# Audio tower on one core: the layers' attention in a new order, and the first stage's maxima subtracted by four wide products

## The reference

```
h = silu(xm @ W_h + b_h) @ W_o + b_o + xm @ W_r + b_r     # xm: 16 samples and 16 ones per token

def _L0_attn_ref(x):                                      # on layernorm(h), 16 heads of 16
    x_centered = xh - jnp.mean(xh, axis=1, keepdims=True)
    corr = jnp.einsum('bthd,bThd->bhtT', x_centered, x_centered)
    corr = jax.nn.softmax(corr, axis=-1)
    out = jnp.einsum('bhtT,bThd->bthd', corr, xh)
h = h + that

def _layer(x, ...):                                       # twice, on layernorm(h); 8 heads of 64
    h = shift_token(x)                                    # columns 128.. come from the token before
    q, k, v = jnp.split(h @ wqkv, 3, axis=-1)
    q = l2norm(q) * qs
    k = l2norm(k) * ksc
    q, k = rotary_xpos(q, k)
    o = local_attention(q, k, v)                          # causal, in a window; softmax(8 q k)
    x = x + o @ wo
    h = layernorm(shift_token(x)) * lg + lb
    a, g = jnp.split(h @ w1 + b1, 2, axis=-1)
    x = x + (a * gelu(g)) @ w2 + b2
h = h + that
```

## Time and profile before

| what | us |
|---|---|
| median of 3 runs (2812.47 to 2817.98) | 2816.48 |
| the profiled execution | 2815.47 |
| its span | 2813.7 |
| TensorE busy | 2682.4 (95%) |
| VectorE busy | 2019.9 (72%) |
| ScalarE busy | 1713.8 (61%) |
| GpSimd busy | 1414.7 (50%) |

### The profile page before, as it was taken

How to read it: one execution, slowest core, us unless ns; L and a number is a source line. 1 busy time by engine, 2 the same in 40 slices (tenths; PEclk the granted TensorE clock), 3 DMA queues, 4 the chain that set the end, 5 groups by cost and what they waited for, 6 DMA issues and landing times.

```text
span 2813.7 us, 68420 instructions
## 1 busy us (share of the span) xinstructions
PE 2682.4 (95%) x23682; PEld 2303.7 (82%) x23808; DVE 2019.9 (72%) x3899; ACT 1713.8 (61%) x4309; POOL 1414.7 (50%) x1337
## 2 busy tenths in 40 slices
PE   6999999968999999997999998999999999899998
PEld 5888888856888888886888886888888888788887
DVE  5666666638888888886755555888888888566664
ACT  3566666536777777775444443777777777444442
POOL 7777777659666666664100004866666666000000
PEclk9999999989999999999999999999999999999999
DMA  1011111021111111111211111111111111222221
GB/s 30 29 34 34 33 33 33 32 80 48 38 36 39 39 39 34 39 39 59 69 56 55 55 57 39 46 39 34 39 39 39 35 38 42 72 78 78 71 78 45
DMA packets 149226, 130.42 MB, mean 46 GB/s; under 512 B 23110, under 2 KB 147304, under 8 KB 149077
## 3 DMA queue, kind: packets, MB, share of 16 engines
q1 hardware_dynamic: 146773, 119.87, 14.1%
q0 software_dynamic: 2304, 8.47, 1.0%
HBM read 77.54 MB, written 50.33 MB: 45 GB/s over the span
## 4 chain that ended last, share of the span: by engine, by line
PE 70%; SPq 2%; DVE 2%; issue 2%; ACT 1%; DMA 0%; POOL 0%; DVEq 0%; ACTq 0%; POOLq 0%
PE const_banks L1292 6%; PE const_banks L1281 6%; PE const_banks L1283 6%; PE const_banks L1294 6%; PE const_banks L1282 6%; PE const_banks L1293 6%; PE const_banks L1375 5%; PE const_banks L1360 4%; PE const_banks L1385 4%; PE const_banks L1348 4%; PE const_banks L1404 3%; PE const_banks L1405 3%; PE const_banks L1406 3%; PE const_banks L1337 2%; PE const_banks L1336 2%; PE const_banks L1335 2%
## 5 line engine op out<-in xcount | busy, mean ns | idle before, releaser
L943 POOL TENSOR_TENSOR attn_qk<-attn_rot_a,attn_rot_b 128x1024 f32<-128x1024 f32 x128 | 364.3, 2846 | 448.3 <-PE const_banks L1348 368.5
L1007 ACT ACTIVATE attn_E<-const_banks,attn_nbias,attn_rn 128x128 f32<-128x128 f32 x1024 | 456.1, 470 | 17.4 <-DVE attn_nbias L1182 17.2
L949 POOL TENSOR_TENSOR attn_rn<-attn_ssm,const_neg_half 128x16 f32<-128x16 f32 x128 | 372.7, 2912 | 16.4 <-DVE attn_ssm L1172 5.5
L930 POOL TENSOR_TENSOR ffn_rstd<-ffn_var,const_neg_half 128x4 f32<-128x4 f32 x32 | 32.3, 1009 | 686.2 <-DVE ffn_var L1107 686.2
L1292 PE MATMUL const_banks<-weights_w_hi,attn_xT_hi 128*128 128x512 f32 x768 | 317.7, 414 | 4.7 <-DVE attn_rot_b L1153 4.1
L1294 PE MATMUL const_banks<-weights_w_hi,attn_xT_lo 128*128 128x512 f32 x768 | 304.0, 396 | 0.0
L1293 PE MATMUL const_banks<-weights_w_lo,attn_xT_hi 128*128 128x512 f32 x768 | 302.4, 394 | 0.0
L1207 DVE SCALAR_TENSOR_TENSOR ffn_gated<-const_banks,weights_b_col,ffn_gate 128x512 f32<-128x512 f32 (+1 forms) x192 | 143.6, 748 | 215.5 <-ACT ffn_gate L1075 208.3
L1281 PE MATMUL const_banks<-ffn_xT_hi,ffn_w_hi 128*128 128x512 f32 x704 | 282.5, 401 | 6.9 <-DVE ffn_xT_lo L1119 5.4
L1283 PE MATMUL const_banks<-ffn_xT_hi,ffn_w_lo 128*128 128x512 f32 x704 | 279.1, 396 | 0.0
L1282 PE MATMUL const_banks<-ffn_xT_lo,ffn_w_hi 128*128 128x512 f32 x704 | 279.0, 396 | 0.0
(11 more groups left out here) (170 smaller groups left out, 7882.8 us busy)
## 6 DMA issues: line engine op xcount, KB each, us to landing
attn_x_<-xa SPq DMA_DIRECT2D x128, 128.0 KB, 2.0
attn_x_res<-xa SPq DMA_DIRECT2D x128, 128.0 KB, 2.1
xb<-attn_x_new SPq DMA_DIRECT2D x128, 128.0 KB, 1.7
ffn_x_<-xb SPq DMA_DIRECT2D x32, 512.0 KB
h<-ident_h SPq DMA_DIRECT2D x64, 128.0 KB, 1.7
xa<-ident_n SPq DMA_DIRECT2D x64, 128.0 KB, 1.7
xa<-ffn_x_new SPq DMA_DIRECT2D x16, 512.0 KB, 3.6
ffn_add<-h SPq DMA_DIRECT2D x16, 512.0 KB, 6.9
```

Source lines behind the costliest of these rows:

```text
L943: pool.tensor_tensor(qk[:, slot].rearrange("p a n -> p (a n)"), rot_a[:].rearrange("p a h d -> p (a h d)"), rot_b[:].rearrange("p a h d -> ...
L949: pool.tensor_tensor(rn[:, slot], ssm[:], c["neg_half"][:], ALU.pow).then_inc(s["rn_done"], 1)
L1007: last = act.activation(E[:, r, i], ps_s[:, r, i * P:(i + 1) * P], ACT.Exp, bias=nbias[:, r, i:i + 1], scale=rn[:, slot, h:h + 1], accum_o ...
```

## The change

Two things are changed.

In the first stage `top` and `topT` become bf16. TensorE turns `top` with a bf16 identity. VectorE, not ScalarE, takes the result out of PSUM: it multiplies it with `pick`, whose column j is -1 on partitions `32k+j` and 0 elsewhere, so that `topT` holds for each j a block that has only its own head's maximum. Four products of 512 columns with ones (`plus`) then subtract. One piece of `row_out` moves ahead of them.

In the layers' attention VectorE rotates before ScalarE squares, both normalisations stand together, and the sums of squares move to the end of VectorE's body; `ssm` is a maximum of two tensors. GpSimd raises k's eight values first, multiplies k, and then raises q's eight. The causal rule is written in four quarters (the lower left one's columns are left out), ahead of the wait for the transposed q and k. The shift by a token is in the load of x, which is two DMAs.

```diff
-        top = n.sb("top", [P, 4, W])
-        topT = n.sb("topT", [P, P])
+        top = n.sb("top", [P, 4, W], BF16)
+        topT = n.sb("topT", [P, 4, P], BF16)
...
-                        act.activation(topT[:], ps_turn[:, 0], ACT.Copy).then_inc(s["mT_ready"], 1)
...
+                        need(dve, s["mT_ps"], b + 1)
+                        need(dve, s["shifted"], b)
+                        dve.tensor_tensor(topT[:], ps_turn[:, 0].unsqueeze(1).to_broadcast([P, 4, P]),
+                                          pick[:].unsqueeze(2).to_broadcast([P, 4, P]), ALU.mult
+                                          ).then_inc(s["mT_ready"], 1)
...
-                        pe.transpose(ps_turn[:, 0], top[:].rearrange("p k w -> p (k w)"), c["ident"][:]
-                                     ).then_inc(s["mT_ps"], 1)
+                        pe.matmul(ps_turn[:, 0], top[:].rearrange("p k w -> p (k w)"), c["ident_b"][:], start=True,
+                                  stop=True).then_inc(s["mT_ps"], 1)
                     if on(OUT):
-                        row_out(t, i, u, 4, 6)
+                        row_out(t, i, u, 4, 7)
...
-                        for j in range(4):
-                            for k in range(4):
-                                own = slice(W * k, W * k + W)
-                                last = pe.matmul(ps_S[:, k, j * P:(j + 1) * P], sel[own, j], topT[own], start=False,
-                                                 stop=(j == 3), skip_group_check=True)
+                        for k in range(4):
+                            own = slice(W * k, W * k + W)
+                            last = pe.matmul(ps_S[:, k], plus[own], topT[own].rearrange("p j t -> p (j t)"),
+                                             start=False, stop=True, skip_group_check=True)
...
-            sp.dma_start(x[:, u % 2], xa[t - layer * ROWS]).then_inc(x_ld[u % 2], 16)
+            row = xa[t - layer * ROWS]
+            sp.dma_start(x[:, u % 2, 0:P], row[:, 0:P]).then_inc(x_ld[u % 2], 16)
+            sp.dma_start(x[1:P, u % 2, P:D], row[0:P - 1, P:D]).then_inc(x_ld[u % 2], 16)
...
-                    pool.tensor_tensor(rn[:, slot], ssm[:], c["neg_half"][:], ALU.pow).then_inc(s["rn_done"], 1)
-                    need(pool, s["rn_done"], b + 1)
+                    pool.tensor_tensor(rn[:, slot, HEADS:], ssm[:, HEADS:], c["neg_half"][:, HEADS:], ALU.pow
+                                       ).then_inc(s["rn_done"], 1)
+                    need(pool, s["rn_done"], 2 * b + 1)
                     need(pool, s["roped"], b + 1)
                     kh = qk[:, slot, 1].rearrange("p (h d) -> p h d", d=HD)
                     pool.tensor_tensor(kh, kh, rn[:, slot, HEADS:].unsqueeze(2).to_broadcast([P, HEADS, HD]),
                                        ALU.mult).then_inc(s["qk_done"], 1)
+                    pool.tensor_tensor(rn[:, slot, 0:HEADS], ssm[:, 0:HEADS], c["neg_half"][:, 0:HEADS], ALU.pow
+                                       ).then_inc(s["rn_done"], 1)
...
+                    need(act, s["rot_b"], b + 1)
+                    need(act, s["normed"], 2 * b - 1)
+                    act.activation(sq[:].rearrange("p h d -> p (h d)"), ps_qk[:].rearrange("p a n -> p (a n)"),
+                                   ACT.Square).then_inc(s["squared"], 1)
...
-                    need(dve, s["squared"], b + 1)
+                    need(dve, s["qk_ps"], b + 1)
...
+                if on(1):
+                    b = t - 1
+                    need(dve, s["squared"], b + 1)
+                    need(dve, s["rn_done"], 2 * b)
+                    dve.tensor_reduce(ss[:], sq[:], AX_X, ALU.add).then_inc(s["normed"], 1)
+                    need(dve, s["normed"], 2 * b + 1)
+                    dve.tensor_tensor(ssm[:], ss[:], tiny[:], ALU.max).then_inc(s["normed"], 1)
...
-                    need(pe, s["rot_a"], b)
-                    need(pe, s["rot_b"], b)
+                    need(pe, s["squared"], b)
...
+                    for r in range(2):
+                        own = slice(r * HD, (r + 1) * HD)
+                        eye, rule = c["ident_b"][own, own], c["causal"][own]
+                        pe.matmul(ps_s[0:HD, r], eye, rule.rearrange("p i n -> p (i n)"),
+                                  start=True, stop=False, skip_group_check=True)
+                        pe.matmul(ps_s[HD:P, r].rearrange("p (i n) -> p i n", n=P)[:, :, HD:P], eye, rule[:, :, 0:HD],
+                                  start=True, stop=False, skip_group_check=True)
                     need(pe, s["qT_done"], b + 1)
                     need(pe, s["kT_done"], b + 1)
-                    need(pe, s["exp_done"], 2 * b)
-                    for r in range(2):
-                        pe.matmul(ps_s[:, r], c["ident_b"][:], c["causal"][:].rearrange("p i n -> p (i n)"),
-                                  start=True, stop=False, skip_group_check=True)
```

89 lines of the change are left out of this document (42 added, 47 removed).

## The result

| what | before | after |
|---|---|---|
| median, us | 2816.49 (2812.47 to 2817.98) | 2832.1 (2824.58 to 2832.66) |
| ratio, with its 95% interval | | 1.0052 (1.0039 to 1.0065) |
| span of the profiled execution, us | 2813.7 | 2830.3 |
| TensorE busy, us | 2682.4 (95%) | 2657.0 (94%) |

The account below looks back on a forecast made before the run. TensorE's own work was taken to bound both stages, with `tok_hid` on VectorE setting first-stage rows after the change. 2815.47 us + 19 (first stage) - 18 (causal rule) + 0 (filling) = 2816 us, range 2796 to 2842.

Parts of the forecast that it names:

- Steady rows of the first stage: First stage's loop: VectorE's wait and copy delay `tok_hid`; rows +0.33, every fourth +0.66, mean +0.41 over 54 bodies, +22 us.
- TensorE loses 0.91 us per row: First stage: sixteen fp32 products (1.11 us) become four wide bf16 ones (0.25); the transposing product saves perhaps 0.05.
- The first stage's ends: First-stage rows before VectorE's division begins and after `tok_hid` ends: the shorter product saves some 0.5 us in four to eight; -3.
- The causal rule: Layers' attention: four quarters side by side take 0.38 us instead of 0.52; 0.14 saved per row, x 128 = -18 us.
- The new order: Layers' attention: reordering the other engines takes nothing off TensorE and counts only if a chain outlasts its row.
- both thin places: Attention: k ready 0.27 us ahead of its transposes, and VectorE's multiplications of E not caught behind GpSimd's addition.
- The load of x: Layers' attention: x in two transfers of 64 KB issued a row ahead; only the stage's first is waited for, 0.1 us.
- Filling and split rows: Layers' first rows: k ready some 2 us sooner, set against 1 to 3 us more waiting beside weight splits; 0 (-4 to +4).
- shorter quarters and a short loop: Faster rival: attention's quarters start together and the first stage's loop is at its short end; 2802 us, chance 0.22.

Follow-up runs that it names:

- e5: e4 with `tok_hid` of a row's first half moved directly behind VectorE's copy, ahead of the statistics; 2772.0 us, 0.9842 of the kernel before.
- e4: The whole change with VectorE's copy of the turned maxima behind the reciprocal and division instead of ahead of them; 2788.0 us, 0.9897 of the kernel before.
- e12: The whole change, but ScalarE writes the turned maxima in four operations instead of VectorE's copy; 2831.1 us, 1.0053 of the kernel before.
- e1: The kernel before with only the first stage's part of the change; 2839.7 us, 1.0084 of the kernel before.
- e2: The kernel before with only the layers' attention part of the change; 2808.7 us, 0.9973 of the kernel before.
- e7: e2 with x loaded in one transfer and the shift by a token back in the copies; 2800.1 us, 0.9942 of the kernel before.
- e11: e3 with x loaded in two transfers, one copy and one subtraction of 256 columns; 2798.8 us, 0.9942 of the kernel before.
- e3: The kernel before with only the causal rule in four quarters, ahead of the wait for q and k; 2797.6 us, 0.9934 of the kernel before.
- e6: e2 with GpSimd's piece of the weight split between the addition and the first power; 2810.6 us, 0.9982 of the kernel before.

## Why the prediction failed, step by step

- **Steady rows of the first stage, +22**: right in the mechanism, with luck in the number. The row that it was worked out from takes 9.02 for 8.97 and the mean loss per row at full clock is 0.37 for 0.41, but the mean is made up otherwise: most rows lose 0.18 where 0.33 stood, those with the three small instructions 0.85 where 0.66 stood. It held in 43 rows, not in 54: in the other eleven `tok_hid` ends 6.60 after the scores and plain rows are 8.68, hardly more than before. That is 15.7 and 1.3 us, 17.0 for 22; and 4.8 came from stretches at TensorE's lower level, which had no term. That the two make 21.8 is chance.
- **TensorE loses 0.91 us per row**: it loses 0.77 (8.64 to 7.87 in e5). The wide products stand for 0.32 instead of 0.25, and the transposing product in bf16 saves nothing where 0.05 stood: from its start to the next line it is 0.03 us before and 0.04 in e5, though its record has 0.27. The Trainium skill, "TensorE: Matmul & The Clock Gate", section "Measured speedup vs the span model", led to an estimate of 0.28: that is nearer to the 0.32. It did not matter here, since `tok_hid` set the row.
- **The first stage's ends, -3**: this is the step that failed most. The term counted only rows in which the shorter product counts, and those it had right: three at the start and the three that take 7.45 us for 8.22 give 3.3 together. It put nothing for the three rows behind them, in which GpSimd splits weights (+5.3), and nothing for the way from there to the first transposes of x (+5.2). GpSimd sets the pace there: its first split ends 26.3 us after the scores of row 57 start, and 26.6 in the change, so what the shorter rows won just before is lost again; its second ends 3.4 later, with 4.2 and 2.9 us of waiting for the division where it waited 1.5 and 1.5. From row 57 to the last one it takes 58.3 us for 55.3; with the copy behind the division (e4) 57.1, with the copy on ScalarE (e12) 55.0. So the copy on VectorE makes that loss, and its place ahead of the division 1.2 of the 3.0. Of the 5.2, 1.9 are in e1 too, which has the old load, and 3.3 come with the new one. e1, without the load's share, has +24.2 for the whole stage where +19 stood.
- **The causal rule, -0.14 per row**: the mechanism right, the size low. Measured 0.19, the stretch 0.34 instead of 0.38. -23.1 where -18 was the sum, with fewer rows than I had multiplied it with.
- **The new order**: right that it takes nothing off TensorE, and both thin places held: slack 0.28 for 0.27, and neither multiplication of E (0.69 each, at 1015.30 and 1016.12) was caught behind GpSimd.
- **The load of x, 0.1 us**: wrong. The term had no row behind it, and it took both transfers to move like one. It stands ahead of all of attention. From its issue to TensorE's first transposes it takes 3.3 to 3.6 us longer in three pairs of kernels (e2 and e7, e11 and e3, the whole change and e1), because 127 packets run one at a time. The medians show 8.6 and 1.2 for the first two pairs.
- **Filling and split rows, 0 (-4 to +4)**: 7.6 us over both layers. That the first k is ready sooner did not pay for the rows with splits; e6 shows that GpSimd's idle time in them is not what costs.

The sum, in its own terms: 17.0 for 22 in the first stage's steady rows, -3.3 for -3 beside them and -23.1 for -18 in attention came out 10.4 us better than forecast. What stood at nothing came to 26.0: lower clock in the first stage 4.8, its last three rows 5.3, the transition 5.2, the first rows of the layers 7.6 and what lies behind layer 1's attention 3.1. The last is in unchanged code, and kernels with 8 to 12 us at the lower level there take 409.5 to 411.3 us for it, those with less than 6 take 408. The rival "shorter quarters and a short loop" had its first half right (0.34 is nearer to 0.31 than to 0.38). None of the rivals named the edges.

What stays open: why the two transfers show 8.6 us under the new order and 1.2 under the old one, when x is late by about the same in both, and what in the new order makes the first rows of a layer longer.
